# A Mamba block between two expert layers: twelve of the second routing's row tiles worked inside the Mamba turns

## The reference

```
x = x + 0.5 * ffn(layernorm(x))      # mixture of 8 experts, 2 chosen for each token, hidden 512
x = x + mamba(layernorm(x))          # selective scan, 64 heads of 8, state 16; mamba(x) holds its own residual
x = x + 0.5 * ffn(layernorm(x))      # the same mixture, same weights

def ffn(x):                                         # x: 4096 tokens
    logits = x @ router_w.T                         # 8 experts
    top_vals, top_idx = top_k(logits, 2); w = softmax(top_vals)
    y[e] = square(relu(x @ w1[e])) @ w2[e]
    return w[0] * y[top_idx[0]] + w[1] * y[top_idx[1]]

def mamba(x):                                       # conv of 4 taps, silu, then for each step t:
    h = h * exp(dt_t * A) + dt_t * x_t * B_t;  y_t = h . C_t
    g = (y + D * xs) * silu(z);  g = g * rsqrt(mean(g * g) + eps) * rms_w
    return x + g @ W_out
```

## Time and profile before

| what | value |
|---|---|
| median of 3 runs | 1088.42 us (1088.01 to 1103.92) |
| profiled execution, its own time | 1089.27 us |
| its span | 1087.4 us |
| busy in the span: PE, DVE, ACT, POOL | 902.4, 881.8, 726.4, 573.4 us |
| granted TensorE clock, mean of the span | 0.947 |

### The profile page before, as it was taken

The page is one execution under the profiler, slowest core; times in us unless marked ns, Lnnn a source line. Parts: engine busy times, 40 slices in busy tenths (PEclk is TensorE's granted clock), DMA queues, the critical chain, the costliest instruction groups (busy, mean ns, idle before and its releaser), DMA issues.

```text
span 1087.4 us, 40975 instructions
## 1 busy us (share of the span) xinstructions
PE 902.4 (83%) x14616; PEld 773.4 (71%) x14616; DVE 881.8 (81%) x2802; ACT 726.4 (67%) x1741; POOL 573.4 (53%) x644
## 2 busy tenths in 40 slices
PE   2228899999989899898999998998942888999990
PEld 1117888998967677676777776876632777889990
DVE  6998884575589899899899998998878788855785
ACT  3454655566679799798899998997633555556650
POOL 4764675566444444445444554443357455755641
PEclk9999999999989999999999999999965889999996
DMA  9944578585346677577676676764522454665997
GB/s 255 303 135 94 128 155 189 102 176 107 88 90 128 113 133 129 109 130 127 118 131 121 130 130 120 130 118 85 96 61 91 100 116 116 146 149 105 192 229 246
DMA packets 186965, 147.44 MB, mean 136 GB/s; under 512 B 106480, under 2 KB 154608, under 8 KB 186640
## 3 DMA queue, kind: packets, MB, share of 16 engines
q0 software_dynamic: 42672, 70.19, 32.1%
q1 hardware_dynamic: 138336, 69.38, 28.6%
q10 hardware_dynamic: 5760, 5.26, 1.7%
HBM read 41.35 MB, written 51.22 MB: 85 GB/s over the span
## 4 chain that ended last, share of the span: by engine, by line
DVE 40%; PE 32%; issue 11%; DMA 5%; SPq 4%; ACT 3%; POOL 3%; DVEq 0%; POOLq 0%; ACTq 0%
PE bank L926 12%; PE bank L939 11%; DVE lake L1213 7%; DVE arena L1267 4%; PE bank L1629 2%; PE bank L1698 2%; POOL disp L753 2%; DVE q_ L1190 2%; SPq L830 2%; DVE lake L1220 2%; ACT lake L1495 2%; DVE lake L1274 2%; DVE lake L1246 2%; DVE lake L1234 2%; DVE arena L1044 1%
## 5 line engine op out<-in xcount | busy, mean ns | idle before, releaser
L926 PE MATMUL bank<-arena,weights 128*128 128x128 f16 x3408 | 221.7, 223 | 15.2 <-DMA arena<-disp 12.9
L871 POOL DMA_INDIRECT ychosen<-arena,didx x142 | 150.9, 1063 | 147.8 <-issue 84.6
L926 PEld LDWEIGHTS bank<-arena,weights 128*128 x3408 | 207.7, 100 | 20.4 <-issue 17.5
L939 PE MATMUL bank<-weights,arena 128*128 x1704 | 212.5, 276 | 10.4 <-DVE arena L1049 9.3
L939 PEld LDWEIGHTS bank<-weights,arena 128*128 128x128 f16 x1704 | 162.5, 99 | 30.1 <-issue 12.3
L980 ACT ACTIVATE arena<-bank 128x512 f32<-128x512 f32 x142 | 84.6, 596 | 134.8 <-PE bank L926 114.7
L1044 DVE TENSOR_TENSOR arena<-arena 128x512 f32<-128x512 f32 x142 | 98.3, 692 | 94.1 <-ACT arena L980 88.7
L753 POOL DMA_INDIRECT disp<-lake,sloti x128 | 133.7, 1045 | 46.6 <-issue 37.5
L1213 DVE SCALAR_TENSOR_TENSOR lake<-lake,vec 128x128 f32<-128x128 f32 x480 | 128.7, 346 | 0.0
L1355 POOL DMA_DIRECT2D lake<-turned_y x32 | 27.8, 869 | 153.8 <-DMA turned_y<-lake 153.8
L1049 DVE TENSOR_TENSOR arena<-arena 128x512 f16<-128x512 f32 x142 | 98.2, 692 | 4.9
(11 more groups left out here) (195 smaller groups left out, 1966.1 us busy)
## 6 DMA issues: line engine op xcount, KB each, us to landing
arena<-in_w SPq DMA_DIRECT2D x16, 512.0 KB, 9.6
yg<-ychosen SPq DMA_DIRECT2D x32, 256.0 KB, 2.9
X<-yg POOLq DMA_DIRECT2D x64, 128.0 KB, 3.6
arena<-lake SPq DMA_DIRECT2D x128, 64.0 KB, 3.3
lake<-lake POOLq DMA_DIRECT2D x32, 256.0 KB, 3.3
turned_y<-lake SPq DMA_DIRECT2D x128, 64.0 KB, 1.9
lake<-turned_y POOLq DMA_DIRECT2D x32, 256.0 KB, 4.1
lake<-ychosen SPq DMA_DIRECT2D x32, 256.0 KB, 4.8
```

The costliest lines, as they stand in the source:

```text
L871: pool.indirect_dma_start(ychosen, bass.IndirectOffsetOnAxis(ap=didx[:, place:place + 1], axis=0), ysb[n % YB][:, :], None).then_inc(S(f"y ...
L926: mm = pe.matmul(o, chunk(where, 2 * ("hl".index(w) * WN + c * HID + m * P), P), v, start=c == 0 and n_ == 0, stop=c == KD - 1 and n_ == 2)
L939: mm = pe.matmul(down_ps(n), x, chunk(where, 2 * ((2 + "hl".index(w)) * WN + c * D), D), start=c == 0 and n_ == 0, stop=c == KH - 1 and n_ ...
```

## The change

The first three groups of the second routing, twelve row tiles, are worked inside the Mamba turns, row tile by row tile, once their output row has been added to `X`:

- Row tile k (0 to 11) has its statistics in turn 2k + 2 (`row_stats`, `row_power`), norm and halves in turn 2k + 3 (`row_norm`, `row_high`, `row_low`), transposes and logits in turn 2k + 4 (`row_turned`, `row_logits`). It lives in a ring of six buffers in the arena instead of the group's buffer.
- Group g (0 to 2) has its two largest picked in turn 8g + 11 (`row_choose`), one-hot and ranks in 8g + 12 (`row_one_hot`, `row_ranks`), slots in 8g + 13 (`row_places`), weights in 8g + 14 (`row_weights`).
- Its scatters leave on POOL from turn 8g + 13 on, two a turn; those of the third group four a turn, in turns 29 and 30 (`rows_leaving`, `row_send`). They stand behind `add_turned` (L1355) and ahead of `add_choice` and `add_out`.
- The table of the first phase is written in turn 31 on DVE, ahead of the statistics of groups 3 and 4. Where turn 31 ended with the first group, it now ends with the fourth (`EG` = 3): its choice, ranks and slots stand ahead of the last gate, as the first group's did.
- The expert functions no longer run the routing up to the fourth group before their first tile. The fifth group's transposes and logits stand behind the first expert tile on PE (`PE_AT`, `ACT_AT`), and the fourth group's eight scatters ahead of the first result's scatter on POOL.
- `gz`, the gate's buffer, is single where it was double. SP's first load of the second layer waits for the last `intra`, and ACT's first square and first copy-out wait for the row tiles' scatters and the last output rows.

Cut to its core, the diff is:

```diff
+EG, RING = 3, 6
+AHEAD = EG * GT_
+ROW_TURN = 2
 TILES = (2 * NT * P + E * (P - 1)) // P
...
+def row_step(i, lag):
+
+    n = i - ROW_TURN - lag
+    return n // 2 if n % 2 == 0 and 0 <= n // 2 < AHEAD else None
+
+
+def group_step(i, lag):
+
+    n = i - ROW_TURN - lag
+    return n // (2 * GT_) if n % (2 * GT_) == 0 and 0 <= n // (2 * GT_) < EG else None
+
+
+def rows_leaving(i):
+
+    turn = {k: 2 * GT_ * (k // GT_) + 11 + (k % GT_ if k < AHEAD - GT_ else k % GT_ // 2) for k in range(AHEAD)}
+    return [k for k in range(AHEAD) if turn[k] == i - ROW_TURN]
...
+        row32 = [carve(ROW // 2) for p in range(RING)]
+        rows16 = [t.bitcast(F16) for t in row32]
...
+            g0, n0, rows0 = groups_before(r), r * NG, AHEAD if r else 0
...
+            first = EG if r else 0
+            if r == 0:
+                start_count(dve)
+            stats(first)
+            stats(first + 1)
+            yield ("stats", first + 1)
...
+            def row_stats(k):
+                if k == 0:
+                    start_count(dve)
+                dve.wait_ge(S("m_xout"), 16 * (k + 1))
+                chain.link(dve.bn_stats(st[:, 0:6], Xk(k)))
+                chain.link(dve.bn_aggr(row(mv, k, 2), st[:, 0:6]))
+                dve.tensor_scalar(row(var, k, 1), row(mv, k, 2)[:, 1:2], EPS, None, ALU.add).then_inc(S("var"), 1)
+
+            def row_norm(k):
+                dve.wait_ge(S("rstd"), NG + k + 1)
+                dve.tensor_scalar(row_xh[:, :], Xk(k), row(mv, k, 2)[:, 0:1], row(rstd, k, 1), ALU.subtract, ALU.mult)\
+                    .then_inc(S("xh"), 1)
+
+            def row_low(k):
+                d = rows16[k % RING]
+                dve.wait_ge(S("hi"), 2 * NG + k + 1)
+                dve.tensor_tensor(d[:, D:2 * D], row_xh[:, :], d[:, 0:D], ALU.subtract).then_inc(S("lo"), 1)
+
+            def row_choose(g, turn):
+                dve.wait_ge(S("logit_ps"), 2 * NG + GT_ * (g + 1))
+                dve.wait_ge(S("m_bt"), turn + 1)
+                chain.link(summed(dve, row_logit_ps))
+                largest(dve, chain, g).then_inc(S("dm"), 1)
+
+            def row_one_hot(g):
+                one_hot(dve, chain, g)
+                dve.sem_inc(S("ohb"), 1)
+
+            def row_places(g, turn):
+                dve.wait_ge(S("rank_ps"), NG + g + 1)
+                dve.wait_ge(S("counted"), (NG + 1) + g + 1)
+                dve.wait_ge(S("m_bt"), turn + 1)
+                ranked(dve, chain, g, row_rank_ps)
+                dve.tensor_tensor(counted[1 - g % 2][:, :], counted[g % 2][:, :], row_rank_ps[:, GT_ * E:(GT_ + 1) * E], ALU.add)\
+                    .then_inc(S("counted"), 1)
+                slots(dve, chain)
+                for j in range(GT_):
+                    m = dve.tensor_copy(row32[(g * GT_ + j) % RING][:, D + 2:D + 3], ixf[:, 2 * j:2 * j + 1])
+                chain.link(m)
+                dve.tensor_copy(row_slots[g][:, :], slotf[:, :]).then_inc(S("slot"), 1)
+
+            def row_weights(g):
+                dve.wait_ge(S("ed"), NG + g + 1)
...
+                if row_step(i, 0) is not None:
+                    row_stats(row_step(i, 0))
+                if row_step(i, 1) is not None:
+                    row_norm(row_step(i, 1))
+                if group_step(i, 9) is not None:
+                    row_choose(group_step(i, 9), i)
+                if group_step(i, 10) is not None:
+                    row_one_hot(group_step(i, 10))
+                if group_step(i, 11) is not None:
+                    row_places(group_step(i, 11), i)
+                if group_step(i, 12) is not None:
+                    row_weights(group_step(i, 12))
+                if inside(i):
                     decays(i, 2)
                 if inside(i - 1):
...
+                    until(table(dve, chain, 1, 0), None)
+                    until(routing, ("stats", EG + 1))
                 if inside(i):
                     gate_in(i)
+                if row_step(i, 1) is not None:
+                    row_low(row_step(i, 1))
                 if inside(i + 1):
...
+            def row_send(k):
+                g, j = k // GT_, k % GT_
+                pool.wait_ge(S("slot"), NG + g + 1)
+                pool.wait_ge(S("lo"), 2 * NG + k + 1)
+                pool.wait_ge(S("tok"), NG + k + 1)
+                hold(pool, "pool")
+                for x in range(2):
+                    pool.indirect_dma_start(disp, bass.IndirectOffsetOnAxis(ap=row_slots[g][:, 2 * j + x:2 * j + x + 1], axis=0),
+                                            rows16[k % RING][:, :], None).then_inc(S(f"row_out_{k % RING}"), 16)
+
...
+                if row_step(i, 0) is not None:
+                    row_power(row_step(i, 0))
...
+                for k in rows_leaving(i):
+                    row_send(k)
...
-                if i == NT:
-                    until(routing, ("sent", 0, 2 * GT_ - 1))
...
+            def row_high(k):
+                d = rows16[k % RING]
+                if k == 0:
+                    all_stored(act, TILES)
+                after(act, f"row_out_{k % RING}", 32 * (k // RING))
+                act.activation(row32[k % RING][:, D:D + 2], const(C_TOK)[:, 2 * k:2 * k + 2], ACT.Copy).then_inc(S("tok"), 1)
+                act.wait_ge(S("xh"), 2 * NG + k + 1)
+                act.activation(d[:, 0:D], row_xh[:, :], ACT.Copy).then_inc(S("hi"), 1)
+
+            def row_turned(k):
+                act.wait_ge(S("xt_ps"), 2 * NG + k + 1)
+                act.wait_ge(S("logit_ps"), 2 * NG + k)
+                act.activation(row_xT[:, :], row_xt_ps, ACT.Copy).then_inc(S("xt"), 1)
...
+            def row_turned(k, turn):
+                pe.wait_ge(S("lo"), 2 * NG + k + 1)
+                pe.wait_ge(S("m_hn"), turn + 1)
+                for c in range(2 * KD):
+                    m = pe.transpose(row_xt_ps[:, c * P:(c + 1) * P], rows16[k % RING][:, c * P:(c + 1) * P], ident16)
+                m.then_inc(S("xt_ps"), 1)
...
+            def row_logits(k, turn):
+                pe.wait_ge(S("xt"), 2 * NG + k + 1)
+                bank_free(turn)
+                j = k % GT_
+                for c in range(2 * KD):
+                    m = pe.matmul(row_logit_ps[:, j * 2 * E:(j + 1) * 2 * E], row_xT[:, c * P:(c + 1) * P],
+                                  rwf[:, c % KD * 2 * E:(c % KD + 1) * 2 * E], start=c == 0, stop=c == 2 * KD - 1)
+                m.then_inc(S("logit_ps"), 1)
+
+            def row_ranks(g, turn):
+                pe.wait_ge(S("ohb"), NG + g + 1)
+                bank_free(turn)
+                counts(pe, ohb[g % 2], row_rank_ps).then_inc(S("rank_ps"), 1)
+
...
+                if row_step(i, 2) is not None:
+                    row_logits(row_step(i, 2), i)
+                if group_step(i, 10) is not None:
+                    row_ranks(group_step(i, 10), i)
+                if group_step(i, 9) is not None:
+                    pe.wait_ge(S("dm"), NG + group_step(i, 9) + 1)
+                if group_step(i, 11) is not None:
+                    pe.wait_ge(S("slot"), NG + group_step(i, 11) + 1)
...
+                 {0: ("logits", 4), 3: ("ranks", 4), 4: ("turned", 5), 5: ("logits", 5), 10: ("ranks", 5), 11: ("turned", 6), 12: ("logits", 6),
...
+                  {0: ("turned", 4), 1: ("rows", 5), 2: ("ratio", 4), 4: ("turned", 5), 9: ("rows", 6), 10: ("ratio", 5), 11: ("turned", 6),
...
+                    if r and s == 0:
+                        sp.wait_ge(S("m_intra"), NT)
```

423 lines of the change are left out of this document (235 added, 188 removed).

## The result

| what | before | after |
|---|---|---|
| median of 20 runs, us | 1089.68 (1077.52 to 1103.92) | 1101.12 (1089.59 to 1115.45) |
| ratio, 95% interval | | 1.0089 [1.0066, 1.0112] |
| profiled execution, its own time; span | 1089.27; 1087.4 | 1100.19; 1098.5 |
| granted clock, mean of the span | 0.947 | 0.951 |

The change makes the kernel 0.9% slower. That is less than the 2% taken as the limit of a single comparison, but with 20 runs of each it is measured. The forecast was 1092.0 and the range 1080 to 1106. The measured time lies above the forecast's own case (1083 to 1099), in the band that I had given to a late POOL (1100 to 1110).

What follows compares the result with a forecast made beforehand. DVE's instructions were taken to bound the Mamba turns, PE close behind, and a dependency chain the routing stretch. 36.5 us of the 38.9 removed are paid back; 1089.3 + 4.2 (clock) - 1.5 (lead) = 1092.0 us, range 1080 to 1106.

Steps and rivals of the forecast that it cites:

- the forecast's own case: Whole kernel: 1092 us, running from 1083 to 1099 with the bounds of the terms; chance 0.57.
- a late POOL: Rival, Mamba turns: scatters delay POOL's work for DVE's norm; 1100 to 1110 in part (0.14), beyond 1110 in full (0.07).
- POOL's powers: Rival, Mamba turns: twelve new powers stop DVE during decays and gate, 8 us, about 1100; chance 0.04.
- the sum: Whole kernel: profiled 1089.3, + 4.2 for the clock, - 1.5 for the lead, gives 1092.0 us.
- The added work: Mamba turns: 1.32 us a row, 5.0 a group, all on DVE's path; turns 30.8 us longer.
- The clock: Turns 12, 20 and 28: PE idles some 2.1 us and its clock falls, 1.4 us each, 4.2 in all.
- The stops: PE stops of about 2.3 us in intra, no wait visible; work ahead of intra only moves them; no term of their own.
- What is moved at the end: Turn 31 to last projection: table delays the last gate 5.7 us, then 16.0 and 6.3 unchanged.
- no Mamba norm is left to wait there: Last two scatter turns: four scatters, 5.0 us, don't fit POOL's gap of 2.65, but no Mamba norm waits for them.
- the second rival: POOL comes late in the Mamba turns through its scatters: 15 us if half counts (0.14), 30 if all (0.07).
- The lead: Expert phase: first tile 2.4 us earlier without the clock's 4.2, growing to 3.0 by PE alone; 1.5 kept to the end.
- DVE's idle time: Rival, turns 2 to 30: half of 35 us idle takes up added work, 1075; given 1076 to 1083, chance 0.14.

Runs made afterwards that it cites:

- before_jump_again: Kernel before the change with PE jumping over no-ops in seven turns, so that no fetch block begins near intra; second run of it: 1067.47 us, ratio 0.9839.
- after_jump: Changed kernel with only nine jumps in PE's stream, putting intra's start at slots 58 to 239 of a 256-instruction fetch block: 1068.89 us, ratio 0.9865.
- after_late_higher: Changed kernel with DVE's group steps behind the fourth decays and ten jumps in PE's stream, intra's lowest slot 78: 1064.07 us, ratio 0.9769.

## Why the forecast was 9 us low

The range held the time; the forecast did not, and that the range reached so far was luck: its upper part stood there for a late POOL and for POOL's powers, and most of the miss came from neither. The profiled execution is 10.9 us slower, and the sum had + 2.7. The turns 2 to 30, from L1310 (or its counterpart) of turn 1 to that of turn 30, cut the difference into its parts. In this order: before, after, `before_jump_again`, `after_jump`, `after_late_higher`.

```profile
334.96:774.09 439.13, 414.92 (x7940) 330.00 (x7937) 401.54 (x1241) 385.02 (x1064) 206.84 (x256) 0.99 0.66 121
```

```profile
332.10:816.54 484.44, 440.44 (x8078) 347.15 (x8075) 429.30 (x1394) 394.19 (x1102) 230.99 (x287) 0.95 0.62 115
```

```profile
332.38:753.04 420.66, 409.53 (x7940) 326.60 (x7937) 400.32 (x1242) 384.28 (x1064) 206.69 (x256) 1.00 0.69 127
```

```profile
333.30:786.62 453.32, 424.32 (x8078) 335.23 (x8075) 427.83 (x1394) 393.93 (x1102) 231.04 (x287) 0.99 0.66 123
```

```profile
336.17:784.78 448.61, 422.18 (x8088) 332.59 (x8086) 427.70 (x1393) 393.71 (x1103) 229.89 (x288) 1.00 0.66 125
```

- **The added work** is what the last has over the third: 448.61 - 420.66 = 28.0 us, where I had 30.8. By turns: 0.86 for statistics and 0.38 for norm and low half, 1.24 a row (I had 1.32); a group, in `after_late_higher`, 0.75 + 1.96 + 1.21 + 0.42 = 4.34 (I had 5.0, with slots and weights too dear). "All of it is on DVE's path" was right.
- **The clock**, together with the idle time of PE ahead of the gate, is what the fourth has over the fifth: 4.7 us, where I had 4.2 for the clock alone. The two kernels differ in the place of the group steps as well as in slots, so the two parts aren't told apart. The dips come in turns 12, 20 and 28 alone, as forecast, once the stops are gone. The busy time of `after_jump` by stretch, turns 12 to 28 (the clock is the third number from the end):

```profile
485.27:502.50 17.23, 14.56 (x271) 11.51 (x269) 16.31 (x59) 13.48 (x39) 7.29 (x10) 0.90 0.56 106
502.50:612.85 110.35, 103.57 (x1972) 81.83 (x1970) 103.49 (x338) 96.94 (x271) 60.31 (x74) 1.00 0.68 129
612.85:630.08 17.23, 14.84 (x273) 11.86 (x271) 16.31 (x59) 13.44 (x39) 7.30 (x10) 0.90 0.59 106
630.08:738.77 108.69, 102.67 (x1970) 81.35 (x1968) 102.62 (x334) 96.80 (x270) 60.30 (x73) 1.00 0.69 132
738.77:755.35 16.58, 14.34 (x267) 11.27 (x265) 15.35 (x55) 12.21 (x36) 6.77 (x9) 0.90 0.55 96
```

They are paid one turn later: turns 13, 21 and 29 take 18.0, 17.5 and 17.5 us, and 16.1, 16.0 and 15.8 in `after_late_higher`, where the group steps leave PE no idle time of 2.3 us ahead of the gate.
- **The stops** are the step that failed. I wrote of them that "work put ahead of `intra` only moves the stop", and kept their number, so that the sum had nothing for them. They cost 439.13 - 420.66 = 18.5 us before and 484.44 - 453.32 = 31.1 after: **12.6 us**, more than the whole miss. That is 3.7 us for each of five and 4.4 for each of seven, their own 1.6 to 2.7 and the clock behind them. By the medians, which come from several chips, it is 10.0 us: 1101.1 - 1068.9 = 32.2 after and 1089.7 - 1067.5 = 22.2 before. The turn behind turn 12's stop took 23.5 us, with a clock of 0.80:

```profile
512.61:536.12 23.51, 21.81 (x330) 17.64 (x326) 15.53 (x55) 15.67 (x44) 6.76 (x9) 0.80 0.45 83
```

The change adds 9.5 PE instructions a turn on average, so that a block boundary falls near `intra` every four turns instead of five, and in its one-hot turns the packet comes late, behind PE's longer wait, at slots 46 and 56. That the wait is what makes it late was read from traces.
- **What is moved at the end** was right: table 834.73 - 829.27 = 5.5 (5.7), and from there to the end of the projection 22.15 (16.0 + 6.3).
- **Turn 31** has a wait that I had not counted ("no Mamba norm is left to wait there"). POOL and DVE, then ACT and PE, behind the first four scatters:

```profile
809.12 1.30 POOL L1506 DMA_INDIRECT disp<-arena,row_slots  x1 [0.30 <-issue]
...
813.46 3.20 POOL L1461 TENSOR_SCALAR mss<-mss 128x1 f32<-128x1 f32 x1
816.86 0.57 POOL L1466 TENSOR_TENSOR mss<-mss,mhalf 128x1 f32<-128x1 f32 x1 [0.21 <-POOL mss L1461]
```

```profile
812.60 4.02 DVE L1284 SCALAR_TENSOR_TENSOR lake<-lake,vec 128x128 f32<-128x128 f32 x15
```

```profile
817.51 0.47 ACT L1701 ACTIVATE xo<-bank,mss 128x256 f32<-128x256 f32 x1 [2.55 <-POOL mss L1466]
```

```profile
818.04 0.64 PE L1842 MATMUL bank<-a,arena 128*128 128x64 f16 x16 [1.85 <-ACT xo L1701]
```

The power of the output norm stands behind the scatters as well. But they made it only somewhat late; most of the wait is one short instruction of POOL, L1461, which took 3.20 us. The other 31 of its kind in this kernel took 0.18 to 0.82. It started 0.86 us into the fifteen instructions of DVE's `conv`, which read two on-chip tensors each, and ended 0.03 us after the last of them. In `after_jump` the same one took 3.60 and ended as `conv` did. In `after_late_higher`, with the same four scatters ahead, it started just ahead of `conv` and took 0.43, ACT didn't wait for POOL there (a wait of 1.9 us came a turn later), and the turn took 18.4 us, with its group steps in another place.

Turn 31 (L1310 of turn 30 to that of 31) takes 22.05 us instead of 14.30, 7.75 more, of which 5.5 are the table: 2.3 us are left for the wait and the lower clock that follows. So the second rival holds in small, in the one place where its price (5.0 us against a gap of 2.65) was over the limit, and most of its price is POOL standing still beside DVE.
- **The lead.** From the first expert matmul to the span's end I had + 0.9 (1.8 later there, 2.7 at the end); it was + 0.05.

Added up at the first expert matmul, against my 847.5: + 12.6 for stops, + 2.05 in turn 31 (7.75 against 5.7), + 0.5 clock, - 2.8 work, - 0.25 behind turn 31, - 2.9 for turns that began earlier. That is + 9.2, and it stood at 856.72.

Of the rivals, DVE's idle time did not take up the work: it grew, in turns 2 to 30 from 37.6 to 55.1 us (439.13 - 401.54, 484.44 - 429.30). POOL came late in a way that cost time only in turn 31. POOL's powers did not hold DVE up. The page's rows of the `decays`, before and after:

```profile
L1267 DVE TENSOR_TENSOR arena<-arena,cb 128x512 f32<-128x512 f32 x128 | 82.4, 684 | 2.8 <-ACT arena L1454 2.8
```

```profile
L1338 DVE TENSOR_TENSOR arena<-arena,cb 128x512 f32<-128x512 f32 x128 | 84.8, 685 | 3.8 <-ACT arena L1603 3.0
```

By the rule of the Trainium skill's page "SBUF — State Buffer", section "SBUF: two separate sides", a DVE operation with two inputs in on-chip memory and a POOL operation that reads it exclude each other, and the one that starts first blocks the other in full. These rows show no `decays` of DVE that got longer. The 3.20 us of L1461 beside `conv` look like the other half of the rule, DVE blocking POOL, though POOL stood through some twelve DVE instructions and the page speaks of one; no run changed that alone.

## What to carry to other kernels

An "issue" stop inside a dense run of short matmuls, at a fixed number of PE instructions from the last one, is the program running out: count the instructions between two stops before you explain them by the work around them. Any change to PE's stream moves these stops, even one of a few instructions a turn, so compare two versions only after each has had its block boundaries kept away from the dense run; here that was worth 22 us to the kernel before and 32 to the kernel after, and the change itself is then 1 us slower, less than these runs can tell from nothing. Work that makes PE wait longer ahead of such a run may cost twice, by the wait and by the later fetch.
